# Attention with a Toeplitz bias: the bias strips of a tile laid into PSUM ahead of its score matmuls instead of added behind them

## The chip, the cores and the metric

One core of one Trainium2 chip. The metric is the device time of one execution in microseconds (us), the median of several runs. The kernel before takes 1925.23 us (three runs, 1925.01 to 1925.26).

## The reference

Input `x` is 4 x 1024 tokens of 512 features. The layer is

```
q, k, v = x Wq.T, x Wk.T, x Wv.T          # 32 heads of 16; rotary embedding on q and k
s[i, j] = q_i . k_j / 4 + bias_h[i - j]   # bias only for 0 <= i - j < 256
s[i, j] = -inf for j > i                  # causal
p = softmax over j with an extra logit offset_h in the denominator
x = layernorm(x + (p v) Wo.T)
x = layernorm(x + fp4_quantised(x) fp4_quantised(W).T + b)
```

The row maximum (with the bias and the offset in it) is taken off before the exponential.

## The kernel before, in words

Three phases. Phase 1 projects and rotates q, k and v and splits q and k into bf16 parts. Phase 3 is the output projection, the two layernorms and the quantised linear layer. The change touches phase 2 only, the attention.

Phase 2 runs over 8 groups of 4 heads and, in each, over 4 batches: 32 group-batches. Scores are computed transposed, keys on the partitions. One batch has 12 tiles T (`TILES`): T = 0 to 3 are the key blocks of the first 512 queries (widths w = 512, 384, 256, 128), T = 4 to 11 those of the last 512 (w = 512 five times, then 384, 256, 128). A tile has two units, u = 2T (heads 0, 1, "even") and u = 2T + 1 (heads 2, 3, "odd"). Each unit owns two PSUM banks of `ps_s`; there are two such pairs and no more, so a unit can be filled only when the exponential of the unit two before has read its banks.

TensorE works through one written order (`phase2`, from line 716), per unit u:

- `scores` (L652): waits for the exponential of unit u - 2 (L657), then two matmuls of w columns (L662), one per head. Between the two and behind them come one or two *maxima* matmuls.
- `maxima` (L640, matmul L649): query-key products for the batch two ahead, up to 512 wide, from which VectorE takes row maxima. There are 48 a batch, dealt out two (sometimes three) per unit to units 0 to 21 (`units_beside`). They go into a ring of 3 PSUM banks (`RING`): a maxima matmul waits until VectorE has read the use three before. I call them m0 to m47.
- behind the odd unit of a banded tile, `add_bias` (L669): 16 matmuls (L677) of 32 output partitions each add the bias, 4 strips for each of 4 heads, up to 384 columns wide, and signal `scored` for both units. The tiles 4 and 5 have no bias; the other ten are `BANDED`. The bias is a Toeplitz band `toep` times a flipped identity, and because it carries -1e30 above the diagonal it is the causal mask too.
- behind that, `pv` (L682, matmuls L691): probabilities times values of the tile before, 8 matmul records of 32 output partitions.
- at u = 1 also `transpose_shift` ("M", L705; VectorE splits it in `split_shifts`, L1151), at u = 4 and 13 `transpose_out` ("O1", "O0", L696; VectorE normalises at L1171 to L1178). M, O1 and O0 take a place in the ring like a maxima matmul.

ScalarE runs one exponential a unit (`exp_unit`, L866, instruction L871) when `scored` says so, and copies the output accumulator (L876) after units 1 and 9. VectorE works on the ring in the ring's order (`max_unit`, L1108): a reduction (L1119), a band operation with the bias (L1126), or both. Each engine runs its own list strictly in order.

Of the kernel before, what the change touches and what calls it, by code (L numbers as in the profile page):

```python
# [46 lines left out]
ROWS = STACK + PARTS  # L47
# [8 lines left out]
STRIP = 32  # L56
# [6 lines left out]
NU = 2 * NT  # L63
# [3 lines left out]
def tile_cols(T):  # L67
    c, J = TILES[T]
    i0 = max(P * J, CH * c)
    return c, J, i0, CH * (c + 1) - i0  # L70


def band_cols(T):

    c, J, i0, w = tile_cols(T)
    b0 = i0 - P * J
    return b0, max(0, min(BAND - b0, w))


BANDED = [T for T in range(NT) if band_cols(T)[1]]  # L80
# [23 lines left out]
def units_beside(u):  # L104

    ks = list(range(min(NM, NM * u // SPREAD), min(NM, NM * (u + 1) // SPREAD)))
    return ks[:1], ks[1:]
# [55 lines left out]
def ahead(g, b, k=AHEAD):  # L163

    return (g, b + k) if b + k < B else (g + 1, b + k - B)
# [7 lines left out]
def slot_free(k, depth):  # L173

    return FIRST + k - depth + 1
# [34 lines left out]
def build(nc, hT, h, wqT, wkT, wvT, woT, bias, bias_rev, offset, wff, bff, cos, sin, out):  # L210
    ctx = ExitStack()
    with ctx:
        def sb(name, shape, dt=FP32):
            return ctx.enter_context(nc.sbuf_tensor(name, shape, dt))

        def sem(name):
            return ctx.enter_context(nc.semaphore(name))
# [13 lines left out]
        q_stack = sb("q_stack", [P, 4, HG, S], BF16)  # L231
# [4 lines left out]
        toep = sb("toep", [PARTS * STRIP, 2, HG, TOEP], BF16)  # L236
        flip = sb("flip", [PARTS * STRIP, STRIP], BF16)
# [40 lines left out]
        ps_s = ps[:, 3:7, :].rearrange("p (r a) t -> p r a t", r=2)  # L278
# [92 lines left out]
        scored = sem("scored")  # L371
        exp_done = sem("exp_done")
# [224 lines left out]
        def _(pe):  # L597
# [37 lines left out]
            def wait_use(use):  # L635

                if not isinstance(use.before, int) or use.before >= RING:
                    pe.wait_ge(ring_read, use.before - RING + 1)

            def maxima(g, b, ks, use_of):  # L640

                for k in ks:
                    I, c0, c1 = MAX_UNITS[k % NMU]
                    hl = k // NMU
                    if k == 0:
                        pe.wait_ge(stack_loaded[b], 16 * 9 * (g + 1))
                    use = use_of(k)
                    wait_use(use)
                    pe.matmul(ps_ring[:, use.bank, 0:c1 - c0], q_stack[0:STACK, b, hl, I * P:(I + 1) * P],  # L649
                              k_stack[0:STACK, b, hl, c0:c1], start=True, stop=True).then_inc(ring_filled, 1)  # L650

            def scores(g, b, n, u, between):  # L652

                c, J, i0, w = tile_cols(u // 2)
                if u == 0:
                    pe.wait_ge(shift_loaded[b], 16 * PARTS * (g + 1))
                pe.wait_ge(exp_done, slot_free(n * NU + u, 2))  # L657
                banded = u // 2 in BANDED

                for hh in range(2):  # L660
                    hl = 2 * (u % 2) + hh
                    mm = pe.matmul(ps_s[:, u % 2, hh, 0:w], k_stack[0:ROWS, b, hl, J * P:(J + 1) * P],  # L662
                                   q_stack[0:ROWS, b, hl, i0:i0 + w], start=True, stop=not banded)
                    if hh == 0:
                        between()
                if not banded:
                    mm.then_inc(scored, 1)

            def add_bias(g, slot, b, T):  # L669

                if T == 0 and b == 0:
                    pe.wait_ge(toep_loaded, 16 * PARTS * (g + 1))
                b0, bw = band_cols(T)
                for hl in range(HG):
                    for a in range(STRIPS):
                        c0 = b0 + STRIP * (STRIPS - 1 - a)
                        mm = pe.matmul(ps_s[STRIP * a:STRIP * (a + 1), hl // 2, hl % 2, 0:bw], flip[:, :],  # L677
                                       toep[:, slot, hl, c0:c0 + bw], start=False, stop=True)
                    if hl % 2:
                        mm.then_inc(scored, 1)  # L680

            def pv(g, b, n, T):  # L682

                c, J, i0, w = tile_cols(T)
                pe.wait_ge(exp_done, FIRST + n * NU + 2 * T + 2)
                if T == 0:
                    pe.wait_ge(v_loaded[b % 2], 16 * (g * 2 + b // 2 + 1))
                if J == 0:
                    pe.wait_ge(o_copied, FIRST + n * 2 + c)
                for hl in range(HG):  # L690
                    mm = pe.matmul(ps_o[VW * hl:VW * (hl + 1), i0 - CH * c:CH],  # L691
                                   v_sb[:, b % 2, J, VW * hl:VW * (hl + 1)], probs[:, T % 3, hl, 0:w],
                                   start=(J == 0), stop=(T + 1 in T_OF_CHUNK))
                mm.then_inc(pv_done, 1)

            def transpose_out(g, b, n, c, last):  # L696
                pe.wait_ge(o_copied, FIRST + n * 2 + c + 1)
                use = Use(g, b, f"O{c}", last)
                wait_use(use)
                for i in range(4):  # L700
                    mm = pe.transpose(ps_ring[:, use.bank, i * P:(i + 1) * P],  # L701
                                      o_sb[:, c, i * P:(i + 1) * P], ident[:, :])
                mm.then_inc(ring_filled, 1)

            def transpose_shift(n, use):  # L705
                pe.wait_ge(shift_steps, 4 * n + 2)
                wait_use(use)
                pe.transpose(ps_ring[0:HG * NB, use.bank, 0:P], shift[:, :], ident[:, :]).then_inc(ring_filled, 1)
# [7 lines left out]
            def phase2(g, slot, last):  # L716
                for b in range(B):
                    n = g * B + b
                    ga, ba = ahead(g, b)
                    more = not (last and b >= B - AHEAD)  # L720

                    def use_of(what):
                        return Use(g, b, what, last)

                    for u in range(NU):
                        inner, behind = units_beside(u) if more else ((), ())
                        scores(g, b, n, u, lambda: maxima(ga, ba, inner, use_of))
                        maxima(ga, ba, behind, use_of)
                        if u % 2 and u // 2 in BANDED:
                            add_bias(g, slot, b, u // 2)  # L730
                        if b and u == PV_LEFT:
                            pv(g, b - 1, n - 1, NT - 1)
                        if u % 2 and u > 1:
                            pv(g, b, n, u // 2 - 1)
                        if b and u == MT_LEFT and not (last and b > B - AHEAD):
                            transpose_shift(n + 1, Use(g, b - 1, "M", last))
                        if b and u == OT_LEFT:
                            transpose_out(g, b - 1, n - 1, 1, last)
                        if u == OT_0:
                            transpose_out(g, b, n, 0, last)  # L740
                    if b == B - 1:
                        if more:
                            transpose_shift(n + 2, use_of("M"))
                        pv(g, b, n, NT - 1)
                        transpose_out(g, b, n, 1, last)

            with pe.Fori(0, G // 2 - 1) as pair:
                for slot in range(2):
                    phase2(2 * pair + slot, slot, False)
            for slot in range(2):  # L750
                phase2(G - 2 + slot, slot, slot == 1)
# [666 lines left out]
```

## Time and profile before

| | us |
|---|---|
| median of 3 runs | 1925.23 |
| profiled execution, its own time | 1923.19 |
| its span on the core | 1921.2 |
| TensorE busy | 1683.8 (88%) |
| VectorE busy | 1276.9 (66%) |
| ScalarE busy | 846.6 (44%) |
| waits of the exponentials (L871) on the bias matmuls (L677) | 587.5 |

Phase 1 runs to about 369 us, then maxima alone to about 420, the 32 group-batches to about 1640, phase 3 to the end. A group (four batches) repeats every 157 us. Engine busy times overlap, so they don't add up; a matmul's recorded length includes its way through the array, so that records of consecutive matmuls overlap and the distance between two starts tells more than the length of one.

### The profile page before, as it was taken

The numbers are of one execution on the slowest core, as the hardware profiler recorded it, in microseconds if no ns is written. First come the engines' busy times: TensorE is split into PE (matmuls) and PEld (weight loads), VectorE is DVE, ScalarE is ACT, GpSimd is POOL, SyncE is SP. The second block draws the span as 40 slices with busy tenths as digits, with TensorE's granted clock in tenths as the row PEclk, the third lists the DMA queues.
The fourth block names the chain that finished last, engine by engine and source line by source line (L and its number), as shares of the span: only waits on it lengthen the run. The fifth ranks groups of instructions, "written<-read, shape, count | busy, mean of one in ns | idle before, by whom it ended". The sixth has DMA issues, their size and how long they took to land.

```text
span 1921.2 us, 40258 instructions
## 1 busy us (share of the span) xinstructions
PE 1683.8 (88%) x12968; PEld 701.0 (36%) x12976; DVE 1276.9 (66%) x3801; ACT 846.6 (44%) x1148; POOL 226.3 (12%) x102
## 2 busy tenths in 40 slices
PE   7999999589989998998998998999899999777772
PEld 3444444123333333333343333333333333333331
DVE  2444444687767776776776776677677770589996
ACT  2333333115544554554554554455455556344442
POOL 4323333300000000000000000000000000034442
PEclk9999999659999998998998999899999999899995
DMA  5444346723332522442335332262235201121111
GB/s 193 159 144 166 134 170 147 183 46 62 54 63 48 96 46 47 81 79 47 66 54 87 58 58 52 49 106 46 46 76 83 47 13 56 50 66 66 66 66 44
DMA packets 123953, 154.70 MB, mean 81 GB/s; under 512 B 15168, under 2 KB 79808, under 8 KB 123488
## 3 DMA queue, kind: packets, MB, share of 16 engines
q1 hardware_dynamic: 123744, 152.11, 34.5%
q8 instruction: 107, 1.75, 0.4%
q14 instruction: 102, 0.84, 0.2%
HBM read 100.78 MB, written 50.50 MB: 79 GB/s over the span
## 4 chain that ended last, share of the span: by engine, by line
PE 53%; issue 19%; DVE 15%; ACT 8%; POOL 3%; DMA 1%; DVEq 1%; ACTq 1%; SPq 0%; POOLq 0%
PE ps L625 12%; PE ps L649 10%; PE ps L662 10%; PE ps L691 9%; PE ps L677 8%; ACT probs L871 7%; DVE mx L1119 4%; DVE junk L1126 3%; PE ps L785 2%; POOL probs L1005 1%; PE ps L701 1%; DVE attn L1178 1%; POOL probs L1036 1%; DVE mx L1126 1%; DMA attn<-wvT 1%
## 5 line engine op out<-in xcount | busy, mean ns | idle before, releaser
L871 ACT ACTIVATE probs<-ps 128x1024 f32<-128x1024 f32 (+3 forms) x768 | 582.8, 810 | 607.9 <-PE ps L677 587.5
L1126 DVE CUSTOM_DVE_ANT_0 junk<-ps,bias_q 128x384 bf16<-128x384 f32 (+2 forms) x1024 | 497.3, 501 | 140.8 <-PE ps L649 127.5
L649 PE MATMUL ps<-k_stack,q_stack 96*128 96x384 bf16 (+3 forms) x1536 | 509.5, 348 | 78.6 <-DVE mx L1126 32.4
L662 PE MATMUL ps<-q_stack,k_stack 99*128 99x512 bf16 (+3 forms) x1536 | 488.0, 336 | 43.8 <-ACT probs L871 24.5
L1119 DVE TENSOR_REDUCE mx<-ps 128x1 f32<-128x128 f32 (+3 forms) x768 | 361.6, 485 | 141.1 <-PE ps L649 140.7
L625 PE MATMUL ps<-attn 128*128 128x512 f32 x768 | 331.7, 595 | 11.4 <-DMA attn<-hT 9.9
L691 PE MATMUL ps<-probs,v_sb 128*32 128x512 f32 (+3 forms) x3072 | 322.9, 496 | 0.8 <-ACT probs L871 0.2
L662 PEld LDWEIGHTS ps<-q_stack,k_stack 99*128 99x128 bf16 x1536 | 142.9, 99 | 367.7 <-ACT probs L871 308.7
L649 PEld LDWEIGHTS ps<-k_stack,q_stack 96*128 96x128 bf16 x1536 | 151.6, 99 | 304.9 <-DVE mx L1126 133.0
L625 PEld LDWEIGHTS ps<-attn 128*128 128x128 f32 x768 | 146.5, 191 | 195.8 <-issue 195.8
L677 PE MATMUL ps<-toep,flip 96*32 96x384 bf16 (+2 forms) x5120 | 214.3, 289 | 0.0
L1036 POOL TENSOR_TENSOR probs<-k_stack,qinv 128x1024 f32<-128x1024 f32 x16 | 30.7, 1917 | 1340.8 <-DVE qinv L1255 1340.8
L785 PE MATMUL ps<-q_stack,k_stack 128*128 128x512 f32 x256 | 120.0, 624 | 23.2 <-ACT k_stack L916 17.4
L1005 POOL TENSOR_TENSOR probs<-attn 128x1024 f32<-128x1024 f32 x32 | 106.2, 3318 | 236.2 <-ACT attn L835 208.0
L677 PEld LDWEIGHTS ps<-toep,flip 96*32 96x32 bf16 x5120 | 98.9, 97 | 84.5 <-issue 62.3
L1079 DVE TENSOR_TENSOR probs<-attn 128x1024 f32<-128x1024 f32 x32 | 39.2, 1225 | 104.0 <-ACT attn L835 92.0
L691 PEld LDWEIGHTS ps<-probs,v_sb 128*32 128x32 f32 x3072 | 80.6, 112 | 28.1 <-issue 9.7
L1126 DVE DVE_READ_ACCUMULATOR2_ANT mx<- 128x1 f32 x1024 | 84.9, 83 | 0.0
L785 PEld LDWEIGHTS ps<-q_stack,k_stack 128*128 128x128 f32 x256 | 49.6, 199 | 84.3 <-issue 63.2
L1085 DVE TENSOR_TENSOR probs<-probs 128x512 f32<-128x512 f32 x32 | 22.6, 705 | 74.6 <-POOL probs L1005 74.6
L1171 DVE TENSOR_TENSOR den<-ps,e_off 128x16 f32<-128x16 f32 x64 | 11.2, 175 | 80.2 <-PE ps L701 80.2
L805 PE MATMUL ps<-bias_q,v_sb 128*128 128x512 bf16 x120 | 39.2, 482 | 19.9 <-ACT v_sb L920 19.7
(86 smaller groups left out, 972.7 us busy)
## 6 DMA issues: line engine op xcount, KB each, us to landing
q_stack<-q_parts SPq DMA_DIRECT2D x192, 128.0 KB, 4.1
v_dram<-v_sb SPq DMA_DIRECT2D x32, 512.0 KB, 2.7
v_sb<-v_dram SPq DMA_DIRECT2D x32, 512.0 KB, 8.9
q_parts<-q_stack SPq DMA_DIRECT2D x96, 128.0 KB, 1.9
k_parts<-k_stack SPq DMA_DIRECT2D x96, 128.0 KB, 2.0
k_stack<-k_parts SPq DMA_DIRECT2D x32, 384.0 KB, 7.4
attn<-hT SPq DMA_DIRECT2D x8, 1024.0 KB, 6.2
k_stack<-k_parts SPq DMA_DIRECT2D x32, 256.0 KB, 8.0
```

The costliest lines, as they stand in the source:

```text
L625: mm = pe.matmul(ps[:, bank, :], lhsT, rhs, start=(kt == 0), stop=(kt == NK - 1))
L649: pe.matmul(ps_ring[:, use.bank, 0:c1 - c0], q_stack[0:STACK, b, hl, I * P:(I + 1) * P], k_stack[0:STACK, b, hl, c0:c1], start=True, stop= ...
L662: mm = pe.matmul(ps_s[:, u % 2, hh, 0:w], k_stack[0:ROWS, b, hl, J * P:(J + 1) * P], q_stack[0:ROWS, b, hl, i0:i0 + w], start=True, stop=n ...
L677: mm = pe.matmul(ps_s[STRIP * a:STRIP * (a + 1), hl // 2, hl % 2, 0:bw], flip[:, :], toep[:, slot, hl, c0:c0 + bw], start=False, stop=True)
L691: mm = pe.matmul(ps_o[VW * hl:VW * (hl + 1), i0 - CH * c:CH], v_sb[:, b % 2, J, VW * hl:VW * (hl + 1)], probs[:, T % 3, hl, 0:w], start=(J ...
L785: mm = pe.matmul(ps_y[:, w, :], at_T[par][:, w, kt * P:(kt + 1) * P], wo_sb[:, kt, :], start=(kt == 0), stop=(kt == NK - 1))
L805: mm = pe.matmul(ps_z[:, w, :], aq_T[par][:, w, kt * P:(kt + 1) * P], wq_T[:, kt, :], start=(kt == 0), stop=(kt == NK - 1))
L871: act.activation(probs[:, (u // 2) % 3, 2 * pr:2 * pr + 2, 0:w], ps_s[:, pr, :, 0:w], ACT.Exp).then_inc(exp_done, 1)
L1005: pool.tensor_tensor(by_sin[:, q % 2, :, :], raw[:, q % 2, :, :], rope_cs[:, 1, q % 2, c:c + 1, :].broadcast_to([P, 2, CH]), ALU.mult).the ...
L1036: pool.tensor_tensor(qs[par].rearrange("p w (q e) -> p (w q) e", e=QBLK), x2[par].rearrange("p w (q e) -> p (w q) e", e=QBLK), qinv[:, par ...
L1119: ins = dve.tensor_reduce(mx[:, par, hl, I, slot:slot + 1], ps_ring[:, use.bank, 0:far], AX.X, ALU.max)
L1126: ins = dve.tensor_tensor_reduce(out=junk[:, use.bank, 0:c1 - lo], in0=ps_ring[:, use.bank, lo - c0:c1 - c0], in1=bias_q[:, hl, BAND - t0 ...
```

## The change

The group loop and all sizes stay. The bias matmuls move: those of tile T + 1 are issued at the end of unit 2T + 1, behind `pv` of tile T - 1 (those of tile 0 at the head of unit 0), with `start=True`. They now wait for the exponentials that last read the two bank pairs: that of unit 2T before the strips of heads 0 and 1, that of unit 2T + 1 before the strips of heads 2 and 3. The score matmuls of a banded tile drop their own wait, cover the full width with `start=False`, and signal `scored` themselves, unit by unit. No maxima matmul stands between the two score matmuls any more. `transpose_shift` of unit 1 comes behind the laying of tile 1's bias.

```
--- before.py
+++ after.py
@@ -649,35 +649,34 @@
                     pe.matmul(ps_ring[:, use.bank, 0:c1 - c0], q_stack[0:STACK, b, hl, I * P:(I + 1) * P],
                               k_stack[0:STACK, b, hl, c0:c1], start=True, stop=True).then_inc(ring_filled, 1)
 
-            def scores(g, b, n, u, between):
+            def scores(g, b, n, u):
 
                 c, J, i0, w = tile_cols(u // 2)
+                banded = u // 2 in BANDED
                 if u == 0:
                     pe.wait_ge(shift_loaded[b], 16 * PARTS * (g + 1))
-                pe.wait_ge(exp_done, slot_free(n * NU + u, 2))
-                banded = u // 2 in BANDED
+                if not banded:
+                    pe.wait_ge(exp_done, slot_free(n * NU + u, 2))
 
                 for hh in range(2):
                     hl = 2 * (u % 2) + hh
                     mm = pe.matmul(ps_s[:, u % 2, hh, 0:w], k_stack[0:ROWS, b, hl, J * P:(J + 1) * P],
-                                   q_stack[0:ROWS, b, hl, i0:i0 + w], start=True, stop=not banded)
-                    if hh == 0:
-                        between()
-                if not banded:
-                    mm.then_inc(scored, 1)
-
-            def add_bias(g, slot, b, T):
+                                   q_stack[0:ROWS, b, hl, i0:i0 + w], start=not banded, stop=True,
+                                   skip_group_check=True)
+                mm.then_inc(scored, 1)
+
+            def lay_bias(g, slot, b, n, T):
 
                 if T == 0 and b == 0:
                     pe.wait_ge(toep_loaded, 16 * PARTS * (g + 1))
                 b0, bw = band_cols(T)
                 for hl in range(HG):
+                    if hl % 2 == 0:
+                        pe.wait_ge(exp_done, slot_free(n * NU + 2 * T + hl // 2, 2))
                     for a in range(STRIPS):
                         c0 = b0 + STRIP * (STRIPS - 1 - a)
-                        mm = pe.matmul(ps_s[STRIP * a:STRIP * (a + 1), hl // 2, hl % 2, 0:bw], flip[:, :],
-                                       toep[:, slot, hl, c0:c0 + bw], start=False, stop=True)
-                    if hl % 2:
-                        mm.then_inc(scored, 1)
+                        pe.matmul(ps_s[STRIP * a:STRIP * (a + 1), hl // 2, hl % 2, 0:bw], flip[:, :],
+                                  toep[:, slot, hl, c0:c0 + bw], start=True, stop=False, skip_group_check=True)
 
             def pv(g, b, n, T):
 
@@ -724,14 +723,17 @@
 
                     for u in range(NU):
                         inner, behind = units_beside(u) if more else ((), ())
-                        scores(g, b, n, u, lambda: maxima(ga, ba, inner, use_of))
+                        if u == 0:
+                            lay_bias(g, slot, b, n, 0)
+                        scores(g, b, n, u)
+                        maxima(ga, ba, inner, use_of)
                         maxima(ga, ba, behind, use_of)
-                        if u % 2 and u // 2 in BANDED:
-                            add_bias(g, slot, b, u // 2)
                         if b and u == PV_LEFT:
                             pv(g, b - 1, n - 1, NT - 1)
                         if u % 2 and u > 1:
                             pv(g, b, n, u // 2 - 1)
+                        if u % 2 and u // 2 + 1 in BANDED:
+                            lay_bias(g, slot, b, n, u // 2 + 1)
                         if b and u == MT_LEFT and not (last and b > B - AHEAD):
                             transpose_shift(n + 1, Use(g, b - 1, "M", last))
                         if b and u == OT_LEFT:
```

## Rows read from the trace of the kernel before

**Rows 1.** The page, its first section: busy us, share of the span.

```profile
PE 1683.8 (88%) x12968; PEld 701.0 (36%) x12976; DVE 1276.9 (66%) x3801; ACT 846.6 (44%) x1148; POOL 226.3 (12%) x102
```

**Rows 2.** Windows: stretch, length, busy PE, PEld, DVE, ACT, POOL, PEclk, DMA.

```profile
1040.00:1079.00 39.00, 34.23 (x294) 13.22 (x294) 23.56 (x86) 16.89 (x21) 0.00 (x0) 0.87 0.31 57
1118.00:1157.00 39.00, 36.31 (x405) 15.14 (x397) 28.98 (x108) 20.33 (x29) 0.00 (x0) 1.00 0.35 61
1525.00:1640.00 115.00, 105.64 (x1197) 40.31 (x1197) 46.12 (x170) 67.80 (x95) 0.00 (x0) 1.00 0.09 29
```

**Rows 3.** Waits in one group, 1040 to 1197 us: total, times, longest.

```profile
ACT probs L871 <- PE ps L677: 77.0, 40, 7.0
PEld ps L662 <- ACT probs L871: 38.3, 67, 1.7
...
PEld ps L649 <- DVE mx L1126: 11.5, 34, 0.6
```

**Rows 4.** Timeline of TensorE, tile 8 of a batch: start us, length, instruction.

```profile
1145.30 0.39 PE L662 MATMUL ps<-q_stack,k_stack 99*128 99x512 bf16 x1
1145.53 0.38 PE L649 MATMUL ps<-k_stack,q_stack 96*128 96x512 bf16 x1
1145.75 0.38 PE L662 MATMUL ps<-q_stack,k_stack 99*128 99x512 bf16 x1
1145.97 0.44 PE L649 MATMUL ps<-k_stack,q_stack 96*128 96x512 bf16 x2
...
1146.70 0.28 PE L649 MATMUL ps<-k_stack,q_stack 96*128 96x256 bf16 x1
...
1147.37 0.34 PE L649 MATMUL ps<-k_stack,q_stack 96*128 96x384 bf16 x1 [0.17 <-DVE mx L1126]
1147.63 0.83 PE L677 MATMUL ps<-toep,flip 96*32 96x384 bf16 x16
1148.29 1.03 PE L691 MATMUL ps<-probs,v_sb 128*32 128x512 f32 x8
1149.35 0.34 PE L662 MATMUL ps<-q_stack,k_stack 99*128 99x384 bf16 x1
```

**Rows 5.** Timeline of VectorE beside it.

```profile
1145.95 0.89 DVE L1119 TENSOR_REDUCE mx<-ps 128x1 f32<-128x512 f32 x2 [1.03 <-PE ps L649]
1146.75 0.55 DVE L1126 CUSTOM_DVE_ANT_0 junk<-ps,bias_q 128x384 bf16<-128x384 f32 x1
1147.23 0.08 DVE L1126 DVE_READ_ACCUMULATOR2_ANT mx<- 128x1 f32 x1
```

**Rows 6.** Timeline of ScalarE beside it.

```profile
1148.27 1.94 ACT L871 ACTIVATE probs<-ps 128x1024 f32<-128x1024 f32 x2 [2.11 <-PE ps L677]
```

**Rows 7.** Timeline of TensorE, the rest of that batch, first and last waits.

```profile
1120.38 0.39 PE L662 MATMUL ps<-q_stack,k_stack 99*128 99x512 bf16 x1
...
1122.90 0.28 PE L708 MATMUL ps<-ident,shift 128*32 128x128 f32 x1
1123.63 0.34 PE L662 MATMUL ps<-q_stack,k_stack 99*128 99x384 bf16 x1 [0.45 <-ACT probs L871]
...
1156.04 0.28 PE L662 MATMUL ps<-q_stack,k_stack 99*128 99x128 bf16 x2
1156.51 0.29 PE L662 MATMUL ps<-q_stack,k_stack 99*128 99x128 bf16 x2 [0.19 <-ACT probs L871]
...
1156.96 0.61 PE L691 MATMUL ps<-probs,v_sb 128*32 128x256 f32 x8
1157.59 0.39 PE L662 MATMUL ps<-q_stack,k_stack 99*128 99x512 bf16 x1
```

**Rows 8.** Timeline of VectorE, the shift split at unit 1.

```profile
1123.22 0.28 DVE L1155 CAST shift_parts<-ps 32x128 bf16<-32x128 f32 x1 [0.20 <-PE ps L708]
...
1124.10 0.28 DVE L1161 TENSOR_TENSOR shift_parts<-shift_rest,shift_parts 32x128 bf16<-32x128 f32 x1
```

**Rows 9.** Timeline of TensorE, first batch of the group.

```profile
1047.30 0.50 PE L662 MATMUL ps<-q_stack,k_stack 99*128 99x384 bf16 x1 [0.57 <-ACT probs L871]
```

## The prediction, made before the change was built or timed

> **What bounds the kernel now.** I read the busy shares first [rows 1]: TensorE is busy 88% of the span, ScalarE 44%. Next the windows, to see whether that holds in phase 2: in a middle batch of a group TensorE is busy 36.3 of 39.0 us at full granted clock, VectorE 29.0, ScalarE 20.3 [rows 2]. Then the waits [rows 3]: the exponentials stand 77 us a group behind the bias matmuls, half of the group. This invites the reading that ScalarE is starved and the bias behind the scores is to blame. But ScalarE has half its time to spare and its idleness costs nothing unless TensorE ends up waiting for it. So the question is how long TensorE, the fullest engine, stands still, and for whom. The waits of the weight loads (38.3 us for the exponentials) don't say it, because the matmuls before still run in that time. That takes the timeline, start to start.
>
> Tile 8 shows the pattern [rows 4]. A 512-wide score or maxima matmul takes 0.22 us of TensorE (starts 1145.53, 1145.75, 1145.97), the 16 bias matmuls 0.66 (1147.63 to 1148.29), the pv matmuls 0.86 by the same measure (four passes of 512 columns at 0.215). Between kinds lie about 0.10. So a 512-wide tile costs 4 x 0.22 for scores, 0.7 to 0.9 for maxima, 0.66, 0.86 and 0.2 of changes, some 3.4 us. It takes 4.05 (1145.30 to 1149.35). The rest are two sorts of wait:
>
> - For the exponential. The next scores at 1149.35 stand behind the even exponential of 1148.27, which with its length of about 1.03 ends at 1149.30: pv was over at 1149.15, with the change of 0.12 that is 0.08 lost.
> - For the ring. m37 starts at 1146.70 and m38 at 1147.37, each right behind VectorE's reading of the use three before: the read that ends at 1147.31 [rows 5] lets m38 go at 1147.37.
>
> I went through all the starts of that batch (1120.38 to 1157.59, 37.2 us [rows 7]) in this way. The exponential costs TensorE 1.92 us in it: 0.52 behind the M transpose (0.11 of matmul and a change of 0.1 after 1122.90, then still until 1123.63), 0.30 at the odd unit of tile 1, 0.36 at 1156.51, 0.08 before 1157.59 [rows 7], and six of 0.03 to 0.24 at tiles 4, 5, 7, 8 (as above) and 9. The ring costs about 3 us. The first is what the change can take away.
>
> **What goes.** No instruction is removed and none added: 160 bias matmuls, 96 scores and 48 maxima a batch before and after, and as many changes between full-width and 32-wide matmuls, since the laying stands directly behind pv as adding stood directly before it. TensorE's own work is the same. The laying of tile T + 1 waits for both exponentials of tile T, but comes later than the old wait, behind pv. In a wide tile the even exponential starts about 0.3 behind its last matmul (1147.63 + 0.33 to 1148.27 [rows 4, 6]); from there to the odd strips TensorE has maxima, the odd scores, maxima, a change, pv and the even strips, 0.4 + 0.43 + 0.4 + 0.1 + 0.86 + 0.33 less that latency, 2.2 or more. The pair of exponentials takes 1.94 [rows 6]. So no wait there. This cover is missing where pv is narrow: at unit 1 it is that of tile 11, 128 wide, 0.21 instead of 0.86. Counted from unit 0's first score, the pair of exponentials starts at 0.43 + 0.3 = 0.73; the even strips can go at 0.73 + 1.03 + 0.05 = 1.81 and end at 2.14, the odd ones at 0.73 + 1.94 + 0.05 = 2.72: 0.58 lost. At the batch's end tile 0's odd strips wait 0.03 for the last exponential (0.66 for the pair, pv 0.43 and strips 0.33 beside it). Of the 1.92 us, 0.6 remain: **-1.30 us a batch**.
>
> **What comes.** The order in a unit was score, maxima, score, maxima; it becomes score, score, maxima, maxima. The first maxima matmul of a tile comes one score later, so VectorE starts later by that, while the end of the tile's last maxima matmul hangs on VectorE. For tile 8, counted from its first score:
>
> - before: m34 at 0.23, VectorE starts 0.42 behind it at 0.65 [rows 4, 5], ends its 0.61 and some 0.1 of release, m37 at 1.40, m38 at 2.07, strips at 2.33, pv, next score possible at 3.97, found at 4.05.
> - after: m34 at 0.43, VectorE at 0.85, m37 at 1.60, m38 at 2.27, its 0.16 and 0.10, pv 2.53 to 3.39, strips of tile 9 to 4.05, next score at 4.15. Slower by 0.10, though the exponential is long done.
>
> The same loss, one score matmul's width, in every tile whose last maxima matmul waits for the ring: tiles 4, 5, 6, 8 (0.22 each), 9 (0.16), 2 and 10 (0.11 each), 1.26 us. Tile 7's wait is set by O0's normalisation and doesn't move; tiles 0, 3 and 11 have no such wait. Bounds of each: nothing (the unit still finds a free bank) and one score's width.
>
> The M transpose is put behind tile 1's strips: it starts at 3.0 behind unit 0's first score instead of 2.52 (1122.90 - 1120.38 [rows 7]). VectorE takes up the split 0.32 after it and needs 1.1 us for it [rows 8], with m4 and m5 queued behind. Before, the 0.7 between M and the next scores covered this; now 0.2 are left. Counted from those scores: split done at 1.20, m4 read at 1.54, m7 can start at 1.68 by its release, TensorE was ready at 1.09. **0.59** lost; bounds 0 and 0.8. What comes is +1.85. SP's loads wait for `scored` of a whole batch, which comes no later; the shift's own load has a batch in hand.
>
> One cost has no row: 32-wide strips straight behind pv (the reverse, strips then pv, shows none: 1147.63 to 1148.29 is 16 matmuls of 384, four side by side, and 0.02). I take 0; the bounds are 0 and 0.10, the change from full to 32-wide, ten times a batch: 0 to +1.0. The Trainium skill (TensorEngine Tiling (Array Packing), Key Properties) says that changing the tiling mode drains the array but changing the tile within it does not; both kinds here are 32 columns wide, and by that the term is 0. No row here shows that transition.
>
> **Sum.** A middle batch: -1.30 + 1.85 = +0.55, 22 of them with maxima outside a group's first: +12. First batches of a group (8): the clock granted is 0.87 over the batch against 1.00 [rows 2], its first tiles run at the lower level after the pause between groups, and there TensorE is too slow to wait for VectorE. Their exponential wait of 0.57 [rows 9] goes and neither M's 0.59 nor tile 2's 0.11 comes; from tile 3 on -1.1 and +1.15. About -0.5 each, -4. The last two batches have no maxima (VectorE 46 of 115 us [rows 2]) and hang on the exponentials: the chain odd exponential, odd strips 0.33, change 0.1, scores 0.43, start 0.3 stands where bias and scores stood, as long as before but for O0's transposes (0.44), which now lie between strips and scores of tile 7 and save little elsewhere: +0.3 each, +0.6. In all +8 us. The profiled execution took 1923.2, so 1931 by it; the median of runs stands 2.0 above that, and I forecast 1933.
>
> **The rivals.**
> - *The ring keeps up* (22%). The head start isn't worth its width, because a maxima matmul queued 0.2 later is only issued in a slot that VectorE would have freed anyway. For it: VectorE idles 10 of 39 us [rows 2] and the ring's entries are short. Against: m38 hangs on the read to within 0.06. Then a batch gains its 1.30, with M's 0.59 perhaps halved: -1.0 to -1.3 over 22, -0.5 to -1.6 over 8: -26 to -41, 1885 to 1900.
> - *The two cancel* (15%): M's delay falls into an idle stretch of VectorE (0 in place of 0.59), the rest as forecast: 22 x -0.04 - 8 + 1, some -5 to +3, 1920 to 1928.
> - *The strips behind pv pay a change* (13%): 0.10 at ten places in 32 batches, +32 over the forecast, 1965; half of it 1949. It decides from 0.03 a place on.
> - *It starves on the odd exponential* is the forecast of one who reads only the new wait: had pv not covered it, 0.6 at every banded tile, +150. Rows 6 against the 2.2 above leave it no place (under 1%).
> - *ScalarE was the bottleneck* (4%): its 2.1 us idle per tile [rows 6] would shrink by the 0.9 of odd scores and strips; ten tiles, 32 batches, -200 or more, 1720. The busy TensorE excludes the most of it: with 3.4 us of own work in a tile of 4.05 the gain ends at 0.3 a tile.
>
> **How the numbers follow.** Forecast 1933 with its own range 1926 to 1948: 46%. This kernel's runs can tell about 0.2%, 3.9 us, from no change. Faster by more: the first rival, the last, and a part of the second, 29%. Within: most of the second and the near edge of the forecast, 16%. Slower: the rest of the forecast and the third, 55%. Range: 1896 cuts off a little over half of the fast cases, 1958 the upper half of the third; together some 20% is left out.
>
> **What would show it.** Right: the exponentials now wait for the scores (L662's lines), as long as before, some 2.2 us in a wide tile, because the start-to-start time of tile 8 stays at 4.1 to 4.2; waits of L649 for VectorE grow by half or more; TensorE stands 0.5 for the odd exponential in the laying of tile 1 and 0.5 for the ring at m7. Strips behind pv follow with no gap. Wrong: if tile 8 takes 3.9 or less, or VectorE's waits do not grow, the first rival holds; if a gap of 0.1 opens between pv and strips, the third.

## The result, and the profile after

The changed kernel takes 1942.86 us (median of four runs, 1942.0 to 1943.45) against 1925.12 (four runs too): a ratio of 1.0092, 95% interval 1.0075 to 1.011. It is slower, as forecast, but by 17.7 us and not by 8, and it lies in the stated range (1896 to 1958).

The page's busy row and the window that answers to the middle batch of [rows 2]:

```profile
PE 1687.0 (87%) x12976; PEld 716.5 (37%) x12976; DVE 1277.6 (66%) x3801; ACT 856.7 (44%) x1148; POOL 226.4 (12%) x102
```

```profile
1118.00:1157.00 39.00, 35.65 (x374) 15.07 (x367) 27.52 (x101) 19.48 (x27) 0.00 (x0) 1.00 0.37 66
```

The instructions are the same as before (12976 weight loads in both; the 12968 matmuls on the page of before are short by a few records), and the clock in this window is 1.00. The waits in the group from 1048 to 1206 us (total us, times, longest):

```profile
ACT probs L873 <- PE ps L663: 79.6, 47, 5.9
...
PEld ps L649 <- DVE mx L1128: 17.2, 36, 0.6
...
PEld ps L649 <- DVE mx L1121: 12.8, 27, 0.8
PEld ps L678 <- ACT probs L873: 10.2, 27, 0.8
...
PE ps L649 <- DVE mx L1128: 4.2, 16, 0.4
```

The exponentials' wait has only changed its partner: 79.6 us for the scores where 77.0 stood for the bias [rows 3]. The waits of the score matmuls for the exponentials are no longer in the list; the wait of the strips for them (10.2) and those of the maxima for VectorE (17.2 and 12.8, and on the matmul itself 4.2) are what stands there now. The row of 11.5 for L1126 in [rows 3] answers to the 17.2 here.

Tile 8 on TensorE (start us, length, instruction), and beside it VectorE's read that lets m38 go, and the exponentials:

```profile
1156.81 0.60 PE L663 MATMUL ps<-q_stack,k_stack 99*128 99x512 bf16 x2
1157.26 0.65 PE L649 MATMUL ps<-k_stack,q_stack 96*128 96x512 bf16 x3
1157.74 0.60 PE L663 MATMUL ps<-q_stack,k_stack 99*128 99x512 bf16 x2
1158.42 0.28 PE L649 MATMUL ps<-k_stack,q_stack 96*128 96x256 bf16 x1
1159.09 0.34 PE L649 MATMUL ps<-k_stack,q_stack 96*128 96x384 bf16 x1 [0.39 <-DVE mx L1128]
1159.36 1.06 PE L690 MATMUL ps<-probs,v_sb 128*32 128x512 f32 x8
1160.24 0.84 PE L678 MATMUL ps<-toep,flip 96*32 96x384 bf16 x16
1161.01 0.50 PE L663 MATMUL ps<-q_stack,k_stack 99*128 99x384 bf16 x2
```

```profile
1158.95 0.08 DVE L1128 DVE_READ_ACCUMULATOR2_ANT mx<- 128x1 f32 x1
```

```profile
1157.53 1.94 ACT L873 ACTIVATE probs<-ps 128x1024 f32<-128x1024 f32 x2 [1.74 <-PE ps L663]
```

From the first score to the next tile's: 1156.81 to 1161.01, 4.20 us against 4.05 [rows 4]. The two scores now run first (1156.81, both in one row), m34 starts at +0.45 instead of +0.23, m37 at +1.61 (before +1.40), m38 at +2.28 (before +2.07), 0.06 after the read that ends at 1159.03. The whole tile has slid by the width of one score matmul, although the exponentials, over at 1159.47, held nobody up.

The stretch around unit 1 on TensorE, with the batch's first score (1130.91) and the next batch's (1169.19), and VectorE's split of the shift:

```profile
1130.91 0.60 PE L663 MATMUL ps<-q_stack,k_stack 99*128 99x512 bf16 x2
...
1132.78 0.51 PE L678 MATMUL ps<-toep,flip 96*32 96x384 bf16 x8
1133.62 0.51 PE L678 MATMUL ps<-toep,flip 96*32 96x384 bf16 x8 [0.33 <-ACT probs L873]
1134.06 0.29 PE L707 MATMUL ps<-ident,shift 128*32 128x128 f32 x1
1134.18 0.49 PE L663 MATMUL ps<-q_stack,k_stack 99*128 99x384 bf16 x2
...
1135.93 0.34 PE L649 MATMUL ps<-k_stack,q_stack 96*128 96x384 bf16 x1 [0.49 <-DVE mx L1121]
...
1169.19 0.61 PE L663 MATMUL ps<-q_stack,k_stack 99*128 99x512 bf16 x2
```

```profile
1134.38 0.28 DVE L1157 CAST shift_parts<-ps 32x128 bf16<-32x128 f32 x1 [0.62 <-PE ps L707]
...
1135.47 0.41 DVE L1121 TENSOR_REDUCE mx<-ps 128x1 f32<-128x256 f32 x1
```

The odd strips of tile 1 stand still from 1133.11 (1132.78 and half of 16 strips, 0.33) to 1133.62, for the odd exponential. M goes at 1134.06, the scores 0.12 later; the split keeps VectorE until 1135.47, and m7 goes at 1135.93, 0.49 late. The batch takes 38.28 us against 37.21 [rows 7].

Of the 20.1 us between the two spans, phase 2 has 16.6: its last copy of the accumulator ends it, and this last copy starts at 1639.6 before and at 1656.2 after (durations min/median/max in ns, first and last start in us):

```profile
L876 ACT ACTIVATE o_sb<-ps x64: 597/605/606, 433.2 to 1639.6; 128x512 f32<-128x512 f32 x64
```

```profile
L878 ACT ACTIVATE o_sb<-ps x64: 597/603/604, 431.7 to 1656.2; 128x512 f32<-128x512 f32 x64
```

The other 3.5 us lie in phase 3, where nothing was changed; among the other kernels below that stretch has either length, so it is not the change's.

The 16.6 us are a balance. A batch is measured from its first score to the next batch's. The batch above is the third of its group and takes 1.07 us more. A second batch takes 1.20 more and a fourth, with the group's end in it, 1.29 or more: the 22 middle batches take 26.7 us more (838.4 to 865.2), 1.21 each. The last two batches add 0.1 and the start 0.8. But the eight first batches of the groups take 11.0 us less (329.0 to 317.9), and that is the clock's doing. Windows over the first batch of the sixth and of the eighth group, before and then after (columns as in [rows 2]):

```profile
1196.80:1239.80 43.00, 37.95 (x351) 14.51 (x348) 26.88 (x97) 18.43 (x25) 0.00 (x0) 0.88 0.30 51
1508.90:1545.10 36.20, 33.68 (x350) 13.16 (x348) 26.65 (x97) 18.38 (x25) 0.00 (x0) 1.00 0.34 60
```

```profile
1209.70:1248.40 38.70, 33.88 (x353) 14.25 (x350) 26.14 (x95) 18.96 (x26) 0.00 (x0) 1.00 0.34 57
1523.80:1560.10 36.30, 33.65 (x352) 14.10 (x348) 26.21 (x95) 19.20 (x26) 0.00 (x0) 1.00 0.37 60
```

In the eighth group, with the granted clock at 1.00 in both kernels, the first batch takes 36.22 before and 36.36 after. In the sixth it takes 43.02 at 0.88 and 38.66 at 1.00. Over all eight the lower level of the clock (1.2 GHz) covers 71 us before and 44 after; length times granted clock, summed, is 293.4 before and 296.0 after. So by this estimate the first batches would have taken a little longer at an equal clock, not shorter. Why the lower stretches are shorter no run shows.

### The profile page after: what moved, and what is told of

The parts are those of the page before. It is cut to its first block, busy times and chain, and to the rows that moved or that the text cites. A ratio compares the mean times of both kernels' runs of the same rounds, so it can differ in the third digit from the quotient of the medians.

```text
span 1941.3 us, 40260 instructions
## 1 busy us (share of the span) xinstructions
PE 1687.0 (87%) x12976; PEld 716.5 (37%) x12976; DVE 1277.6 (66%) x3801; ACT 856.7 (44%) x1148; POOL 226.4 (12%) x102
## 3 DMA queue, kind: packets, MB, share of 16 engines
q8 instruction: 107, 1.75, 0.4%
## 4 chain that ended last, share of the span: by engine, by line
PE 57%; issue 17%; DVE 17%; POOL 3%; ACT 3%; DVEq 1%; DMA 1%; ACTq 0%; SPq 0%; POOLq 0%
PE ps L690 14%; PE ps L625 12%; PE ps L649 10%; PE ps L663 8%; PE ps L678 8%; DVE mx L1121 6%; DVE junk L1128 3%; ACT probs L873 2%; PE ps L700 2%; PE ps L787 2%; POOL probs L1007 1%; DVE mx L1128 1%; POOL probs L1038 1%; DMA attn<-wvT 1%; DVE stats L1301 1%
## 5 line engine op out<-in xcount | busy, mean ns | idle before, releaser
L873 ACT ACTIVATE probs<-ps 128x1024 f32<-128x1024 f32 (+3 forms) x768 | 590.0, 810 | 611.0 <-PE ps L663 610.0
L649 PE MATMUL ps<-k_stack,q_stack 96*128 96x384 bf16 (+3 forms) x1536 | 454.7, 345 | 119.1 <-DVE mx L1128 57.4
L663 PE MATMUL ps<-q_stack,k_stack 99*128 99x512 bf16 (+3 forms) x1536 | 377.5, 333 | 1.3 <-ACT probs L873 1.3
L690 PE MATMUL ps<-probs,v_sb 128*32 128x512 f32 (+3 forms) x3072 | 332.1, 504 | 0.1
L678 PE MATMUL ps<-toep,flip 96*32 96x384 bf16 (+2 forms) x5120 | 219.3, 284 | 20.0 <-ACT probs L873 13.1
L678 PEld LDWEIGHTS ps<-toep,flip 96*32 96x32 bf16 x5120 | 125.6, 97 | 209.6 <-issue 112.1
L663 PEld LDWEIGHTS ps<-q_stack,k_stack 99*128 99x128 bf16 x1536 | 119.9, 98 | 122.3 <-issue 69.2
L690 PEld LDWEIGHTS ps<-probs,v_sb 128*32 128x32 f32 x3072 | 60.7, 108 | 68.6 <-issue 42.2
```

What stands on the lines that cost most here:

```text
L873: act.activation(probs[:, (u // 2) % 3, 2 * pr:2 * pr + 2, 0:w], ps_s[:, pr, :, 0:w], ACT.Exp).then_inc(exp_done, 1)
```

## The experiments

Each is compared with the kernel of before on the same chip. "Batch" is the distance of the first scores of two following batches inside a group.

**e1, M in front of the laying.**

```diff
+ transpose_shift(...)                 # u == 1
  if u % 2 and u // 2 + 1 in BANDED:
      lay_bias(g, slot, b, n, u // 2 + 1)
- transpose_shift(...)
```

> The changed kernel with the M transpose put back in front of the laying of tile 1's bias (unit 1). Theory A (VectorE is held up by the late M and then by the late first maxima matmul of each tile): tile 1 of the batches that have an M goes back from 3.45 us by 0.4 to 0.6, about -9 us in all, 1934. Theory B (what costs is the place of the strips, a change of the array between pv and the 32-wide strips at ten places a batch): nothing, 1942 to 1943.

1931.7 us, ratio 1.003 (1.002 to 1.004): 11 below the changed kernel. Its batch, on TensorE:

```profile
1124.80 0.60 PE L663 MATMUL ps<-q_stack,k_stack 99*128 99x512 bf16 x2
...
1162.38 0.60 PE L663 MATMUL ps<-q_stack,k_stack 99*128 99x512 bf16 x2
```

37.58 us, 0.70 less than 38.28. M's place costs what the forecast said and a little more. The 22 middle batches give 15.1 us; the groups' first batches, which have no M in them, give 4.0 back (317.9 to 321.9) with the lower clock in them for 52 us in place of 44.

**e2, one maxima matmul back between the two scores.**

```diff
      mm = pe.matmul(ps_s[...], start=not banded, stop=True)
+     if hh == 0: maxima(inner)
```

> The changed kernel with one maxima matmul back between the two score matmuls of a unit; the laying stays where it is. Theory A: the waits of the maxima for VectorE lose one score's width in eight of twelve tiles, 1.2 us a batch, 30 batches: -36 us, about 1906, below the kernel of before. Theory B: the waits aren't the loss, 0 to -5 us, 1938 or more.

1913.6 us, ratio 0.994 (0.9923 to 0.9958): 29 below the changed kernel, and faster than before. Its TensorE, with the batch's ends and tile 8:

```profile
1112.25 0.39 PE L663 MATMUL ps<-q_stack,k_stack 99*128 99x512 bf16 x1
...
1137.47 0.39 PE L663 MATMUL ps<-q_stack,k_stack 99*128 99x512 bf16 x1
1137.70 0.38 PE L649 MATMUL ps<-k_stack,q_stack 96*128 96x512 bf16 x1
...
1139.54 0.34 PE L649 MATMUL ps<-k_stack,q_stack 96*128 96x384 bf16 x1 [0.17 <-DVE mx L1129]
1139.80 1.07 PE L692 MATMUL ps<-probs,v_sb 128*32 128x512 f32 x8
1140.68 0.84 PE L680 MATMUL ps<-toep,flip 96*32 96x384 bf16 x16
1141.45 0.34 PE L663 MATMUL ps<-q_stack,k_stack 99*128 99x384 bf16 x1
...
1149.37 0.39 PE L663 MATMUL ps<-q_stack,k_stack 99*128 99x512 bf16 x1
```

The batch takes 37.12 us, 1.16 less than 38.28; tile 8 takes 3.98, m34 at +0.23 and m38 at +2.07 as in the kernel of before. Tile by tile the changed kernel stands above e2 by 0.22, 0.21, 0.15 and 0.22 in tiles 4, 5, 6 and 8, by 0.16 in 9 and 0.11 in 2 and 10: the list of the prediction but for 0.07 in tile 6. Theory A is right, though 36 us were expected of it and 29 came; theory B, by which this could not matter, falls.

**e3 and e4, VectorE made light** in the kernel of before and in the changed one: it reads 32 columns of each maxima matmul, so the maxima are incomplete.

```diff
- ps_ring[:, use.bank, 0:far]
+ ps_ring[:, use.bank, 0:32]
```

> The kernel of before, VectorE reading only 32 of the up to 512 columns of each maxima matmul (the maxima are left incomplete). The ring then never holds TensorE; what is left of waiting is for the exponentials. Both theories: faster by 2 to 3 us a batch, about 1925 - 75 = 1850.

> The changed kernel, VectorE reading only 32 columns of each maxima matmul (the maxima are left incomplete). Against the same cut in the kernel of before: theory A, faster than it by the exponential's waits of 1.3 us a batch and more, 25 to 50 us, near 1815; theory B, not faster than it, since the loss has nothing to do with VectorE.

1840.6 (ratio 0.956, 0.9538 to 0.9582) and 1808.2 (0.9391, 0.937 to 0.9413). With VectorE light the same change is worth 32 us in the good direction. The ring is not quite gone: in a middle batch of e3 TensorE still stands about 1.0 us at it, of 3.1 before. Of the 32 us only 12.4 lie in the 22 middle batches (0.57 each, 34.93 to 34.26 in a third batch); 19.4 lie in the groups' first batches (308.3 to 289.0), part of them by a higher granted clock. The sign in the middle batches, -0.57 here and +1.21 with VectorE at its full work, hangs on the ring.

**e5, both mendings.**

> Both mendings at once: M in front of the laying, one maxima matmul between the two score matmuls. If the two losses are separate, as theory A has them, their gains add: 1913.6 less the 11 of M alone, about 1903. If they are one loss (VectorE's backlog counted twice), 1910 or more.

1890.1 us, ratio 0.9828 (0.981 to 0.9846), 13 better than expected. The kernel of before took 1925.4 on the chip of e1 and e2 and 1923.9 on this one; against it, M's place is worth 22 here and 11 in e1.

```profile
1100.36 0.39 PE L663 MATMUL ps<-q_stack,k_stack 99*128 99x512 bf16 x1
...
1136.71 0.39 PE L663 MATMUL ps<-q_stack,k_stack 99*128 99x512 bf16 x1
```

In a middle batch it is as good as additive: 36.35 us, 0.77 less than e2 and 1.23 less than e1. The surplus lies in the groups' first batches, and it is the clock again. From e2 to e5 the 22 middle batches give 17.6 us (15.1 in e1) and the eight first ones 7.4 (313.9 to 306.5), where e1 had lost 4.0. M stands in none of them; the lower clock covers 56 us of them in e2 and 40 in e5. Length times granted clock is 285.8 and 286.4.

**e6, also O0's transposes in front of the laying of tile 7.**

> As e5, and O0's transposes in front of the laying of tile 7 instead of behind it. VectorE gets O0 0.44 earlier, and m32, which waits for that bank, too: theory A, 0.3 to 0.4 us a batch, 30 batches, and 0.4 in the two without maxima: 10 us below e5. If m32's wait doesn't decide, no change.

1886.9 us, ratio 0.9814 (0.9795 to 0.9832). The intervals of e5 and e6 overlap, so the time shows no gain; the batch is 0.19 shorter than e5's, half of what was expected:

```profile
1091.68 0.39 PE L663 MATMUL ps<-q_stack,k_stack 99*128 99x512 bf16 x1
...
1127.84 0.39 PE L663 MATMUL ps<-q_stack,k_stack 99*128 99x512 bf16 x1
```

**e7, as e5 but the laying in front of pv.**

> As e5, but the laying in front of pv in place of behind it. The prediction says that pv's 0.86 us cover the laying's wait for the odd exponential. Without it that wait stands open in the wide tiles, 0.4 to 0.6 each, and is partly paid by VectorE catching up: +2 to +4 us a batch against e5, 1965 to 2030. If the cover doesn't matter, equal to e5. The trace also shows what strips cost straight behind a maxima matmul and pv straight behind strips, against 0.88 from pv to strips and 0.77 from strips to scores.

2029.8 us, ratio 1.0551 (1.0528 to 1.0575), 140 above e5. The cover is real. In this kernel even the narrow strips of tile 6 stand 0.62 us for the odd exponential:

```profile
1151.06 0.30 PE L680 MATMUL ps<-toep,flip 96*32 96x128 bf16 x8 [0.62 <-ACT probs L874]
```

**e8, the kernel of before without a maxima matmul between the scores.**

> The kernel of before with only one thing of the change: both maxima matmuls of a unit behind the two score matmuls, nothing else moved. Theory A: VectorE's head start of one score's width goes in eight tiles, 1.2 us a batch, part of it falling into the wait for the exponential that is there anyway: +20 to +38 us, 1945 to 1963. Theory B: nothing.

1961.8 us, ratio 1.0201 (1.0184 to 1.0218), +38. Nothing else of the change is in it.

```profile
1103.00 0.61 PE L662 MATMUL ps<-q_stack,k_stack 99*128 99x512 bf16 x2
...
1141.50 0.61 PE L662 MATMUL ps<-q_stack,k_stack 99*128 99x512 bf16 x2
```

38.50 us a batch, 1.29 more than 37.21. The head start alone costs more than the whole change does.

**e9 and e10, exponentials over half the columns**, in the kernel of before and in the changed one (half of the probabilities is stale).

```diff
- act.activation(probs[..., 0:w], ps_s[..., 0:w], Exp)
+ act.activation(probs[..., 0:w // 2], ps_s[..., 0:w // 2], Exp)
```

> The kernel of before with exponentials over half the columns of each unit (the other half of the probabilities is left stale): the wait for the exponential goes without anything being moved. If that wait is worth what the forecast took (1.9 us a batch, 1.3 of it reached by the change), -1.9 a batch and more in the two batches without maxima, -65 us, 1860. If part of it only turns into a wait for VectorE, as a comparison of e5 with before suggests, -1.2 a batch, -45, 1880.

> The changed kernel with the same half-width exponentials. Only the wait of tile 1's odd strips (0.5 us a batch) and the exponential-bound last two batches are left to gain: -15 to -25 us, 1918 to 1928, so some 40 us above e9: the wait for the exponential has gone from both, and what stands between them is M, the head start and the place of the strips. If ScalarE were still the bottleneck of the changed kernel, its 2 us of idleness per wide tile would shrink and it would gain as much as e9 does.

1879.2 (ratio 0.9768, 0.9751 to 0.9785) and 1923.1 (0.9996, 0.9983 to 1.0008). As in the second half of e9's expectation: 45, not 65. Its TensorE, with m7 of a batch:

```profile
1097.70 0.39 PE L662 MATMUL ps<-q_stack,k_stack 99*128 99x512 bf16 x1
...
1102.08 0.34 PE L649 MATMUL ps<-k_stack,q_stack 96*128 96x384 bf16 x1 [0.29 <-DVE mx L1119]
...
1133.77 0.39 PE L662 MATMUL ps<-q_stack,k_stack 99*128 99x512 bf16 x1
```

The batch takes 36.07, 1.14 less than 37.21, though TensorE stood 1.92 for the exponentials in it. Of the 45 us, 8.9 lie in the last two batches (57.9 to 49.0), of e10's 19 us 9.5. At m7 one sees why: where the kernel of before waited for the odd exponential in tile 1, this one waits for VectorE. A wait taken away in front of the ring's slot is partly waited again at the ring. e10 sits 44 above e9 with the exponential's wait out of both: M, the head start and the strips' place by themselves (38.6 in the 22 middle batches).

**e11, the maxima matmul first, then the score** (built on e6).

```diff
- score, maxima, score, maxima
+ maxima, score, maxima, score      # banded tiles
```

> Built on e6: in banded tiles the order of a unit becomes maxima, score, maxima, score, so that VectorE starts one score matmul's width earlier still. Theory A: another 0.8 to 1.2 us a batch, 25 to 35 us below e6, about 1855. If the ring is no longer what holds TensorE in e6, or its waits in front of the scores hold these up, no gain or a loss.

1917.4 us, ratio 0.9968 (0.9956 to 0.9981), 30 above e6: a miss. Tile 8 and tile 5 on TensorE:

```profile
1105.61 0.39 PE L649 MATMUL ps<-k_stack,q_stack 96*128 96x512 bf16 x1
...
1107.62 0.38 PE L665 MATMUL ps<-q_stack,k_stack 99*128 99x512 bf16 x1
...
1109.59 0.39 PE L649 MATMUL ps<-k_stack,q_stack 96*128 96x512 bf16 x1
...
1133.65 0.28 PE L649 MATMUL ps<-k_stack,q_stack 96*128 96x256 bf16 x1 [0.38 <-DVE mx L1126]
1133.77 0.38 PE L665 MATMUL ps<-q_stack,k_stack 99*128 99x512 bf16 x1
```

In tile 8 nothing is gained (1105.61 to 1109.59, 3.98, as in e2), and no other banded tile is shorter than in e6. The reason, as I argue it: what the first maxima matmul gains in front, the score that now follows the last one (1107.62) takes at the end. The head start counts only for work that still lies between the first and the last maxima matmul. It loses in tiles 4 and 5 (0.21 and 0.40), which have no bias and in which my edit put up to two maxima matmuls between the scores, and 0.14 in tile 7: in tile 5 the last score waits at 1133.77 behind a ring wait of 0.38. The two profiles are 38 us apart: 18.7 lie in the 22 middle batches, 16.5 in the groups' first ones (305.2 to 321.7), where the lower clock covers 63 us in place of 43.

## Why the prediction was right or wrong

Point by point, for the third batch of a group; forecast +0.55, measured +1.07 (+1.21 in the mean of the 22):

| step of the prediction | forecast | measured | from |
|---|---|---|---|
| M behind the strips | +0.59 | +0.70 to +0.77 | after - e1, e2 - e5 |
| the head start | +1.26 | +1.16 to +1.23 (+1.29 in the old order) | after - e2, e1 - e5 (e8) |
| what goes, with the strips' place | -1.30 + 0 | -0.86 | e5 - before |

- **Where the time goes.** Right. TensorE's own waits decide, not ScalarE's idleness: the 77 us became 79.6 and tile 8 takes 4.20 where 4.15 was worked out. Half-width exponentials take 45 us from the kernel of before (e9) and only 19 from the changed one (e10), as was expected of them.
- **The ring takes the place of the exponential.** Right in kind, shown from four sides (e2, e4, e5, e8), and its two causes, M and the head start, have the sizes given them (the table above).
- **The cover of pv.** Right: e7. The forecast for unit 1, 0.58 of waiting, was met with 0.51.
- **The step that failed is "what goes", -1.30 us a batch.** With both costs mended away (e5) only 0.86 of it is left. Two things are missing from it. The first is a wait of the old kernel booked at its full length, whereas part of it only moves to the ring: e9 takes away nearly all of the 1.92 and gets 1.14. I had seen it coming for tile 9 when I gave it a head start loss, but did not take the return off the gain. The second is TensorE's own work, taken as unchanged. Here are the same batches of five kernels taken apart start to start (us; an estimate: own work is the shortest distance that these kernels show between two instructions of the same kinds and widths, and what goes beyond it is a wait; by this count the wait for the exponential before is 2.1, by the prediction's 1.92):

| third batch of the fifth group | length | own work | waits for the exponential | waits at the ring |
|---|---|---|---|---|
| before | 37.2 | 31.9 | 2.1 | 3.1 |
| changed | 38.3 | 32.1 | 0.6 | 5.6 |
| e5 | 36.4 | 32.3 | 0.6 | 3.5 |
| e9 | 36.1 | 31.9 | 0.3 | 3.9 |
| e10 | 37.7 | 32.1 | 0.1 | 5.6 |

  The wait for the exponential did go, by 1.5 and not 1.3. From before to e5, 0.3 of that came back at the ring and 0.4 as own work. Of the changed kernel against before the ring took 2.4, where 1.85 was booked: 0.3 is that return, and 2.1 come with M and the head start. In e9 0.8 of 1.9 came back. Of the own work, part is the term taken as 0, strips straight behind pv. From the last maxima matmul to the next tile's first score the kernel of before needs 1.88 in tile 9:

```profile
1150.77 0.33 PE L649 MATMUL ps<-k_stack,q_stack 96*128 96x384 bf16 x1
...
1152.65 0.28 PE L662 MATMUL ps<-q_stack,k_stack 99*128 99x256 bf16 x1
```

  e2 needs 1.91 in tile 8 (1139.54 to 1141.45) for the same strips and pv in the other order. That is 0.03 here. Over the whole batch, strips and pv together take 13.75 us in the old order (e9) and 13.99 in the new one (e10), with the exponential's wait out of both: 0.24, or 0.024 a place. It is inside the bounds of 0 to 0.10 and just under the price from which that rival was said to decide. The rest of e5's 0.4 is mostly M, which costs TensorE 0.2 more between pv and the strips than behind them.
- The rest of the 0.52 that the batch is off is M (0.11 to 0.18 more than forecast; 0.07 of it is that m7 started 1.75 behind its scores, not 1.68), less 0.03 to 0.10 of head start.
- **The rest of the batches.** Forecast +0.3 each for the two without maxima; the last two exponential pairs of the same kind in them stand 0.35 further apart than before (28.96 for 28.61), and from their first score to the last accumulator copy they take 58.0 us for 57.9. The groups' first batches were forecast to gain 4 us in all, by a wait for the exponential that goes. They gained 11.0, by the clock and not by that wait. This was luck: it hid part of the miss. The 22 middle batches are off by 15 us (+26.7 for +12), the total by 10 only.
- **The rivals.** "The ring keeps up" is refuted by e2 and e8, "the two cancel" by e1 and by m7's 0.49 of waiting. "The strips pay a change" came to 0.24 us a batch, some 8 us of the run, not 32. "Starving on the odd exponential" is what e7 shows for the laying in the other place: +140, near the +150 worked out. "ScalarE was the bottleneck" fell: the time went up, and e10 gains less than e9.
- **Two sums.** The terms of the forecast make 8.6, which was booked as 8. By the 3.4 us of own work in a tile of 4.05 the last rival's gain would end at 0.65 a tile, not at 0.3. Neither changes the account.

The mechanism was right; the net is a small difference of two large terms (about -34 and +52 us of the run: e5 against before, the changed kernel against e5, each against before on the same chip), and an error of a tenth in each is half as large as the result. That should have widened the forecast's own range upward. And a stretch at the lower clock can be worth as much as the term under study: it has to be compared apart, batch by batch.

## What to carry to other kernels

Ask of the full engine, start to start, for whom it stands still; the idle time of a half-empty engine is no measure. When several waits follow each other on one in-order engine, a wait removed is not a gain until the next one in the same period has been checked, for the later one may give it back. And when instructions are regrouped, look at who starts work on the first of them: here one matmul of 0.22 us moved in front of the feeding one costs 1.2 us a batch, while the same change with that order kept is 0.6% faster than before (e2), and 1.9% with M and O0's transposes in front of the laying too (e6).

## What the runs showed that I had not expected

Moving M, a single small transpose, out from behind eight waiting strips is worth 11 us in one order and 22 in the other, though a middle batch gains 0.70 and 0.77: the difference lies in the groups' first batches, where the granted clock was another. The same holds for 11 us of the change itself. And phase 3, the same instructions in every kernel, took 281.6 us in one profile and 285.1 in another; a comparison of two single profiles carries that.
